# Attention scores in two blocks of two slots on four score banks, five other results on two shared banks

## What is computed

```
q = (x @ Wq).reshape(8, 512, 16, 64)      # k and v likewise
scores = einsum('bqhd,bkhd->bhqk', q, k) / 8 + bias[h, q, k]     # bias by relative position
attn = softmax(scores, axis=-1)
ctx = einsum('bhqk,bkhd->bqhd', attn, v).reshape(8, 512, 1024)
x = layernorm(x + ctx @ Wo)
```

## Time and profile before

| what | value |
|---|---|
| median of 3 runs | 2526.76 us (2526.72 to 2529.57) |
| the profiled execution, its own time | 2530.65 us |
| its span in the trace | 2528.9 us |
| first attention, its steps | about us 23 to 1084 of the span |
| busy, whole span | PE 78%, PEld 60%, DVE 68%, ACT 47%, POOL 28% |
| granted TensorE clock, mean of the span | 0.898 of full speed |
| matmuls of a score slot, mean of one | 429 ns, 1536 of them |

### The profile page before, as it was taken

The page is one execution under the profiler, slowest core; times in us unless marked ns, Lnnn a source line. Parts: engine busy times, 40 slices in busy tenths (PEclk is TensorE's granted clock), DMA queues, the critical chain, the costliest instruction groups (busy, mean ns, idle before and its releaser), DMA issues. The chain is left out here.

```text
span 2528.9 us, 36610 instructions
## 1 busy us (share of the span) xinstructions
PE 1960.4 (78%) x11740; PEld 1514.0 (60%) x11741; DVE 1707.1 (68%) x3758; ACT 1181.0 (47%) x2603; POOL 697.4 (28%) x820
## 2 busy tenths in 40 slices
PE   6999999999999999933866046999899988223780
PEld 4777777777777777733755035777677767123670
DVE  5888888888888888835544795775577555666124
ACT  5777777777777777720432323332233222300221
POOL 0111111111111111112855353441234210204681
PEclk9999999999999999966988577999999999656895
DMA  6000000000000000030544100000000000001542
GB/s 195 1 1 1 1 1 1 1 1 1 1 1 1 1 1 1 1 94 4 110 108 86 36 8 1 0 0 1 1 0 0 1 3 1 5 1 37 141 97 71
DMA packets 62347, 64.29 MB, mean 25 GB/s; under 512 B 6145, under 2 KB 51665, under 8 KB 62081
## 3 DMA queue, kind: packets, MB, share of 16 engines
q1 hardware_dynamic: 51186, 44.32, 5.7%
q0 software_dynamic: 11024, 18.23, 4.3%
HBM read 41.89 MB, written 20.38 MB: 25 GB/s over the span
## 5 line engine op out<-in xcount | busy, mean ns | idle before, releaser
L278 POOL TENSOR_TENSOR x<-x,scaled 128x512 f32<-128x512 f32 x128 | 165.0, 1289 | 899.1 <-DVE scaled L529 899.1
L517 DVE TENSOR_TENSOR probT<-turn_ps,probT 128x512 fp32r<-128x512 f32 x512 | 346.4, 687 | 81.2 <-ACT probT L435 71.9
L445 ACT ACTIVATE prob<-prob,negmax 128x512 f32<-128x512 f32 x512 | 371.1, 725 | 61.4 <-DVE negmax L512 57.4
L435 ACT CAST probT<-turn_ps 128x512 fp32r<-128x512 f32 x512 | 297.3, 581 | 128.6 <-PE turn_ps L333 128.5
L512 DVE CUSTOM_DVE_ANT_0 prob<-score_ps,bias 128x512 f32<-128x512 f32 x512 | 332.4, 687 | 1.8 <-issue 1.8
L333 PE MATMUL turn_ps<-ident,prob 128*128 128x128 f32 x2048 | 291.1, 280 | 39.1 <-DVE probT L517 34.5
L333 PEld LDWEIGHTS turn_ps<-ident,prob 128*128 128x128 f32 x2048 | 223.8, 141 | 137.4 <-DVE probT L517 101.6
L345 PE MATMUL ctx_ps<-probT,val 128*128 128x512 f32 x1024 | 270.4, 406 | 0.0
L323 PE MATMUL score_ps<-k,q 64*128 64x512 f32 x1536 | 249.4, 429 | 5.0 <-DVE negmax L512 3.6
L345 PEld LDWEIGHTS ctx_ps<-probT,val 128*128 128x128 f32 x1024 | 177.9, 188 | 61.8 <-issue 23.0
L323 PEld LDWEIGHTS score_ps<-k,q 64*128 64x128 f32 x1536 | 125.6, 186 | 82.1 <-issue 35.2
(11 more groups left out here) (502 smaller groups left out, 4303.2 us busy)
## 6 DMA issues: line engine op xcount, KB each, us to landing
ew<-L_ffn_fc_weight SPq DMA_DIRECT2D x32, 256.0 KB, 3.4
bias<-bias_line SPq DMA_DIRECT2D x16, 448.0 KB, 10.5
mid_rows<-row SPq DMA_DIRECT2D x24, 256.0 KB, 2.5
last_rows<-row SPq DMA_DIRECT2D x24, 128.0 KB, 2.4
rows_dram<-rows SPq DMA_DIRECT2D x1, 2304.0 KB, 9.4
acc_dram<-zero POOLq DMA_DIRECT2D x1, 2112.0 KB, 15.2
acc<-acc_dram SPq DMA_DIRECT2D x1, 2112.0 KB, 10.6
x_rows<-x SPq DMA_DIRECT2D x1, 2048.0 KB, 9.6
```

The lines of the kernel that those rows point to most:

```text
L278: pool.tensor_tensor(mine, mine, scaled[a][:, :, :], ALU.add).then_inc(added, 1)
L435: act.copy(probT[0][:, g % QT, :], turn_ps[g % 2][:, :]).then_inc(turned_hi, 1)
L445: act.activation(prob[p][a][:, i, :], prob[p][a][:, i, :], ACT.Exp, bias=negmax[p][:, i, a:a + 1], scale=-1.0, accum_out=total[p][:, i, a: ...
L517: dve.tensor_tensor(probT[1][:, g % QT, :], turn_ps[g % 2][:, :], probT[0][:, g % QT, :].bitcast(F32), ALU.subtract).then_inc(turned_lo, 1)
```

## The change

Nothing that is computed changes, and no instruction is added or removed but waits. Three things do.

1. Banks. Scores get four banks, `score_ps[i % 2][a]`: slots 0 and 2 use one pair, 1 and 3 the other. Turns keep two. Everything else shares two banks, `work_ps`: V's first piece, the rows, Q and both contexts use `work_ps[0]`; V's second piece, K and both outputs use `work_ps[1]`. (Every `misc_ps`, `ctx_ps` and `out_ps` in the helpers is replaced so; these lines are left out below.)
2. Waits on PE that the shared banks need.
3. The order of the lists:

- PE: S0, S1, T0, T1, V, O1, T2, T3, Q, K, S2, S3, C0, T4, T5, O0, T6, T7, C1
- ACT: c1, exp, exp, t0, exp, t1, exp, v, t2, t3, q, k, exp, exp, exp, c0, t4, exp, t5, t6, t7
- DVE: sc, sc, sc, sc, rt0, rt1, rv, inv, sh1, rt2, rt3, rq, rk, sc, sc, sc, sc, rt4, rt5, sh0, rt6, rt7

```diff
-        score_ps, turn_ps = [bank("score_ps0"), bank("score_ps1")], [bank("turn_ps0"), bank("turn_ps1")]
-        misc_ps = [bank("misc_ps0"), bank("misc_ps1")]
-        ctx_ps, out_ps = bank("ctx_ps"), bank("out_ps")
+        score_ps = [[bank(f"score_ps{i}_{a}") for a in range(2)] for i in range(2)]
+        turn_ps, work_ps = ([bank(f"{n}{i}") for i in range(2)] for n in ("turn_ps", "work_ps"))
...
             def scores(s, p, i):
                 if i == 0:
                     pe.wait_ge(qk_lo, 2 * s + 2)
-                if after(s, 1) or i >= 1:
-                    pe.wait_ge(scored, 8 * s + 2 * i)
+                if after(s, 1) or i >= 2:
+                    pe.wait_ge(scored, 8 * s + 2 * i - 2)
                 for n, (u, v) in enumerate(PASSES):
                     for a in range(2):
-                        mm = pe.matmul(score_ps[a][:, :], q[p][u][head(a), tile_of(i)], k[p][v][head(a), :], start=(n == 0), stop=(n == 2))
+                        mm = pe.matmul(score_ps[i % 2][a][:, :], q[p][u][head(a), tile_of(i)], k[p][v][head(a), :], start=(n == 0), stop=(n == 2))
...
             def step(s, b, r, last):
                 p, back, earlier = r % 2, s - 1, s - 2
                 now, turns, sums = is_step(s), after(s, 1) and is_step(back), after(s, 2) and is_step(earlier)
                 br = (r - 1) % PAIRS
+                ahead = now and not (last and r == PAIRS - 1)
                 if now:
                     scores(s, p, 0)
+                    scores(s, p, 1)
                 if turns:
                     turn(back, 1 - p, 0)
                     turn(back, 1 - p, 1)
                 if now:
+                    if sums:
+                        pe.wait_ge(ctx_ready, 2 * earlier + 2)
                     for n, m in value_pairs(r):
+                        if m == 1:
+                            pe.wait_ge(scaled_ready, 2 * earlier + 1)
                         make_values(b, n, m)
                     if r == PAIRS - 1 and not last:
                         turn_rows(b + 1)
+                    if r == PAIRS - 2:
+                        pe.wait_ge(val_lo, PAIRS * b + PAIRS)
                 if sums:
                     add_head(earlier, b if r >= 2 else b - 1, (r - 2) % PAIRS, 1)
-                if now:
-                    scores(s, p, 1)
                 if turns:
                     turn(back, 1 - p, 2)
                     turn(back, 1 - p, 3)
-                if now and not (last and r == PAIRS - 1):
+                if ahead:
                     if r == PAIRS - 1:
                         pe.wait_ge(x_lo, b + 2)
-                    elif r == PAIRS - 2:
-                        pe.wait_ge(val_lo, PAIRS * b + PAIRS)
-                    else:
+                    elif r < PAIRS - 2:
                         pe.wait_ge(val_lo, PAIRS * b + r + 1)
-                    project(misc_ps[1], wq, (r + 1) % PAIRS)
-                    project(misc_ps[0], wk, (r + 1) % PAIRS)
+                    project(work_ps[0], wq, (r + 1) % PAIRS)
+                    if sums:
+                        pe.wait_ge(scaled_ready, 2 * earlier + 2)
+                    project(work_ps[1], wk, (r + 1) % PAIRS)
                 if now:
                     scores(s, p, 2)
+                    scores(s, p, 3)
                 if turns:
+                    if ahead:
+                        pe.wait_ge(qk_lo, 2 * (s + 1) + 1)
                     context(back, br, 0)
                     turn(back, 1 - p, 4)
                     turn(back, 1 - p, 5)
-                if now:
-                    scores(s, p, 3)
-                if turns:
+                    if s == 1:
+                        pe.wait_ge(wo_in, 32)
+                    if ahead:
+                        pe.wait_ge(qk_lo, 2 * (s + 1) + 2)
+                    add_head(back, b if r >= 1 else b - 1, br, 0)
                     turn(back, 1 - p, 6)
                     turn(back, 1 - p, 7)
-                    if s == 1:
-                        pe.wait_ge(wo_in, 32)
-                    add_head(back, b if r >= 1 else b - 1, br, 0)
                     context(back, br, 1)
...
                     copy_context(earlier, 1)
                 if now and after(s, 2):
                     act.wait_ge(inv_ready, s - 1)
-                for i in range(2):
-                    for a in range(2):
-                        if turns:
-                            turn(back, 2 * i + a)
-                        if now:
-                            exps(s, p, i, a)
-                    if now and i == 0:
-                        for n, m in value_pairs(r):
-                            copy_values(b, n, m)
-                        if r == PAIRS - 1 and not last:
-                            copy_rows(b + 1)
-                    if now and i == 1 and not (last and r == PAIRS - 1):
-                        copy_qk(s + 1, 1 - p, 0)
-                        copy_qk(s + 1, 1 - p, 1)
+                if now:
+                    exps(s, p, 0, 0)
+                    exps(s, p, 0, 1)
                 for a in range(2):
+                    if turns:
+                        turn(back, a)
                     if now:
-                        exps(s, p, 2, a)
-                    if turns:
-                        turn(back, 4 + a)
+                        exps(s, p, 1, a)
+                if now:
+                    for n, m in value_pairs(r):
+                        copy_values(b, n, m)
+                    if r == PAIRS - 1 and not last:
+                        copy_rows(b + 1)
+                if turns:
+                    turn(back, 2)
+                    turn(back, 3)
+                if now and not (last and r == PAIRS - 1):
+                    copy_qk(s + 1, 1 - p, 0)
+                    copy_qk(s + 1, 1 - p, 1)
+                if now:
+                    exps(s, p, 2, 0)
+                    exps(s, p, 2, 1)
+                    exps(s, p, 3, 0)
                 if turns:
                     copy_context(back, 0)
-                for a in range(2):
-                    if turns:
-                        turn(back, 6 + a)
-                    if now:
-                        exps(s, p, 3, a)
+                    turn(back, 4)
+                if now:
+                    exps(s, p, 3, 1)
+                if turns:
+                    turn(back, 5)
+                    turn(back, 6)
+                    turn(back, 7)
...
                     dve.wait_ge(turn_done, 8 * (s - 1))
-                for i in range(2):
-                    if now:
+                if now:
+                    for i in range(2):
                         score(s, p, i, 0, 2 * r)
                         score(s, p, i, 1, 2 * r + 1)
-                    if sums and i == 1:
-                        scale_head(earlier, (r - 2) % PAIRS, 1)
-                    if turns:
-                        rest_of_turn(back, 2 * i)
-                        rest_of_turn(back, 2 * i + 1)
-                    if i == 0:
-                        if now:
-                            for n, m in value_pairs(r):
-                                rest_of_values(b, n, m)
-                            if r == PAIRS - 1 and not last:
-                                rest_of_rows(b + 1)
-                        if turns:
-                            invert(back, (r - 1) % PAIRS)
+                if turns:
+                    rest_of_turn(back, 0)
+                    rest_of_turn(back, 1)
                 if now:
-                    score(s, p, 2, 0, 2 * r)
-                    score(s, p, 2, 1, 2 * r + 1)
-                    if not (last and r == PAIRS - 1):
-                        rest_of_qk(s + 1, 1 - p, 0)
-                        rest_of_qk(s + 1, 1 - p, 1)
+                    for n, m in value_pairs(r):
+                        rest_of_values(b, n, m)
+                    if r == PAIRS - 1 and not last:
+                        rest_of_rows(b + 1)
+                if turns:
+                    invert(back, (r - 1) % PAIRS)
+                if sums:
+                    scale_head(earlier, (r - 2) % PAIRS, 1)
+                if turns:
+                    rest_of_turn(back, 2)
+                    rest_of_turn(back, 3)
+                if now and not (last and r == PAIRS - 1):
+                    rest_of_qk(s + 1, 1 - p, 0)
+                    rest_of_qk(s + 1, 1 - p, 1)
+                if now:
+                    for i in range(2, 4):
+                        score(s, p, i, 0, 2 * r)
+                        score(s, p, i, 1, 2 * r + 1)
                 if turns:
                     rest_of_turn(back, 4)
                     rest_of_turn(back, 5)
-                if now:
-                    score(s, p, 3, 0, 2 * r)
-                    score(s, p, 3, 1, 2 * r + 1)
-                if turns:
+                    scale_head(back, (r - 1) % PAIRS, 0)
                     rest_of_turn(back, 6)
                     rest_of_turn(back, 7)
-                    scale_head(back, (r - 1) % PAIRS, 0)
+
```

(30 more changed lines are left out.)

## The result

The changed kernel takes 2715.72 us (median of 4 runs, 2710.38 to 2718.78), the kernel before 2526.74 us beside it. The ratio is 1.0749, with a 95% interval of 1.0723 to 1.0774: slower by 189 us. The forecast was 2697 us, with 2655 to 2748 around it.

What follows compares the result with a forecast made beforehand. No engine was quite full, so order decides; after the change a cycle through PE, DVE and ACT bounds the step. 2530.65 + 162.4 for steps + 8 for the clock = 2701, less 3.9 to the median: 2697 us, range 2655 to 2748.

Steps and rivals of the forecast that it cites:

- The step that carried the forecast: In ordinary attention steps, copies wait behind exponentials on ACT, delaying DVE, PE and next scores: 18.75 us, 2.39 more.
- The sum: First attention's 63 steps plus its ends: 31.8 us from eight long steps, 129.1 from 54 others, 1.5 from the last: +162.4.
- The ordinary step: Attention step from S0 to the next S0, without two V pieces: 18.75 us forecast against 16.36 before.
- The long step r = 6: One of eight steps with two V pieces; O1 waits for both, PE idle 3.6 us: 20.91 us against 16.93.
- the walk: Model of one step: each instruction starts once its engine is free and inputs are there; gave 16.36 on the old lists.
- The clock term: PE clock may halve after the 3.6 us hole in each of eight long steps: 0 to 13 us, 8 taken.
- Rival C: Clock falls in ordinary steps too: +47 us if in each second step, +95 if in every; 2745 to 2795 us; chance 0.08.
- Worth nothing in itself: Four score banks: S1 need not wait for sc of S0, but that wait was already hidden; only makes the new order possible.
- The edges: Score blocks on PE: two blocks less a step save 0.4 us, or 0.6 if the matmul before is stretched too.
- The 0.2 for a lone slot: A score slot's three matmul pairs take 0.69 us but alone hold PE 0.89, so 0.20 goes at its edges.
- A (PE profits): Rival: PE stays the bound, a step loses edges and at best its holes, 15.9 to 14.9 us, 2500 to 2435; chance 0.04.
- B, a closer phase: Rival: ACT or DVE finds a phase closing one of two holes, 17.5 us a step, +75, 2602 us; chance 0.06.

Runs made afterwards that it cites:

- experiments 5 and 6: Each exponential cut to the first 256 of 512 columns: in the changed kernel 2603.22 us, in the kernel before 2499.17 us.
- experiment 1: Changed kernel with only the ACT and DVE lists reordered, copies first and exponentials late: 2483.4 us, ratio 0.982 to the kernel before.
- experiments 3 and 4: Changed kernel with ACT's order edited, copies ahead of some exponentials, in a step's first half only (2655.6 us) or second half only (2682.74 us).
- with fillers: Changed kernel plus useless PE matmuls in its waits before T2, T3, Q and, in steps r = 6, O1: 2691.1 us, ratio 1.0661.
- experiments 1 and 10: ACT and DVE reordered, copies first, exponentials late: on the changed kernel 2483.4 us; on the kernel before, its banks and PE order kept, 2477.77 us.
- experiment 8: Kernel before with its banks kept, all three lists reordered, copies first, exponentials and key projection late, T0 ahead of S0: 2464.97 us, ratio 0.9754.
- experiment 2: Changed kernel's banks and waits with the order of the kernel before on all engines: 2804.89 us, ratio 1.1102.

## Why the prediction was right, and where it was off

- **The mechanism.** The step that carried the forecast was that t0, v, c0 and t4 stand behind exponentials on ACT, that DVE, PE and the next scores follow from them in turn, and that a step so takes 18.75 us. The trace has each start within 0.15 us of it, experiments 5 and 6 show ACT's exponentials on the path after the change and hardly on it before, and experiment 1 shows that the order on ACT and DVE is a sufficient cause. That it is ACT's order only is not shown: experiments 3 and 4 undo parts of it and gain 0.4 to 0.5 us a step each, and the run that won all of it changed DVE's list too.
- **The size without the clock.** The sum was +162.4 us for the steps. Measured: +183.3, of which 28 is the clock, so 155. The ordinary step was 0.14 us too long (18.61), mostly in its tail from O0 on, 8 us over 54 steps. The long step r = 6 was right where the clock stays up: 20.91 us by the walk, and 20.98 with fillers (S0 at 585.80 and at 606.78). One reason in it was not: sc after S2 was put at 12.24 although S2 at 10.90 and its 1.14 give 12.04, with k said to be subtracted before. With fillers rk starts 0.61 ahead of that sc (597.58 and 598.19), so DVE's queue and not S2 sets it.
- **The clock term.** This was mis-sized: 8 us taken, 13 as its upper end for the steps r = 6, 28 measured; the range, which let the term go 25 us above the 8, held it. Falls were expected after the holes of r = 6 only. They came there in every case (22.0 from reciprocal to reciprocal in an ordinary batch, where 20.4 is the figure with fillers), and in three of the eight steps the clock stayed down for longer: these took 23.6 to 23.9 from S0 to S0, the five others 22.4 to 22.6. Against 20.98 the eight make some 16 us, so 13 was too low a bound even for them. They also came in nine other steps, which took 19.7 to 19.9 from S0 to S0 in place of 18.61; 9 x 1.2 makes 11 us more. One of the nine, T2, T3 and Q, with the clock before and after:

```profile
333.07 0.66 PE L333 MATMUL turn_ps<-ident,prob 128*128 128x128 f32 x4 [0.42 <-DVE probT L531]
334.25 0.66 PE L333 MATMUL turn_ps<-ident,prob 128*128 128x128 f32 x4 [0.53 <-DVE probT L531]
335.44 1.09 PE L305 MATMUL work_ps<-xT,wq_hi 128*128 128x512 f32 x2 [0.53 <-DVE val L516]
```

```profile
331.60:335.40 3.80, 2.36 (x18) 1.69 (x16) 2.54 (x6) 3.80 (x11) 0.00 (x0) 1.00 0.01 2
335.60:339.00 3.40, 3.40 (x10) 2.27 (x12) 2.44 (x5) 1.21 (x3) 1.28 (x1) 0.50 0.00 0
```

Rival C was right for one ordinary step in six or so, not for each second. The Trainium skill, "TensorE: Matmul & The Clock Gate", A second HAM failure mode: psum-queue depth-cycling, says of another kernel that micro-idles between groups of matmuls make the clock swing; this case agrees, in holes of 0.4 to 0.7 us three in a row.
- **The four score banks.** "Worth nothing in itself" fits: experiments 1 and 10 differ by 6 us, no more than their intervals.
- **The edges.** 0.4 us a step was the gain; 1.59 for a block of two agrees. The 0.2 for a lone slot was too small, by experiment 8: with what the work ahead of it loses it is 0.3.
- **The rivals.** A (PE profits) was the wrong way for this order, but not out of reach: a step of 15.4 us, inside its 14.9 to 15.9, was had by other lists. B, a closer phase, did not occur: 37 of the 63 intervals lie between 18.60 and 18.66, and none is shorter but the last, before the pipeline empties.

The median is 19 us above the forecast. Two errors of the sum partly cancel, which is luck: +13 from the steps (28 and not 8 for the clock, 155 and not 162 for the rest), -3.5 from the rest of the span (180 and not 183), and +9 since the profiled execution lay 3.9 us above its median before and lies 5.3 below it now (2710.38).

Left open: that experiment 2 came 50 us above its expectation is put down to the clock. Its 27 steps of 21.0 to 21.2 beside those of 19.63 make some 42 of the 50, but no run with fillers was made of it. Why the clock fell in nine ordinary steps and not in the others, with the same holes, is not shown.

## What to carry to other kernels

When engines work through lists in fixed order, walk one period with starts and handovers from the trace, and check the walk on the old lists first: here it gave the new period within 1%. An engine that is idle a third of the time can still set the period, by what its list puts ahead of the work that others wait for; put copies that free a bank or feed the busiest engine first, and work that is needed only in the next period last (experiments 1, 8 and 10). More buffers, and fewer changes of mode on the busiest engine, are worth little while such an order stands, and each bank that is shared asks for a place in the order of every engine that reads it.

## What the runs showed of the hardware beyond expectation

The granted clock fell to 1.2 GHz in nine steps other than r = 6. The longest idle time on PE just before such a fall was 0.73 us by the rows. In the step shown above T2, T3 and Q waited 0.42, 0.53 and 0.53 us within 2.8 us, and PE did two times four transposes between them. Matmuls of no use, five in those gaps of an ordinary step and twelve in the hole of r = 6, kept it at 2.4 GHz (granted 1.00) in all 63 steps that the reciprocals span, and made the kernel 25 us faster, though they lengthened an ordinary step by 0.12 us.
